# Conv stage: channel-block pairs stored with the low quarter first, only that quarter split in two parts, and the last three tap groups closed row by row

## The reference, cut to what matters

```python
def _L0_attn_a_ref(x, block_values, cols, rows):      # x: (2, 512, 256); 128 blocks of 64 x 64 x 16 taps
    xb = x.reshape(batch, n_block_row, bs, t)          # 8 blocks of 64 channels
    x_unfold = xb[:, cols].reshape(batch, n_blocks * bs, t)
    o = conv_general_dilated(x_unfold, W, padding=[(ks - 1, 0)], feature_group_count=n_blocks)
    y = zeros(...).at[:, rows].add(o)
...
x = x + _L0_attn_a_ref(_layernorm(x), block_values, cols, rows)
x = x + _L0_ffn_ref(_layernorm(x), ...)
x = x + _L0_attn_b_ref(_layernorm(x), ...)
x = x + _L0_ffn_ref(_layernorm(x), ...)
```

## Time and profile before

| what | value |
|---|---|
| median of 3 runs | 882.07 us (882.04 to 882.12) |
| profiled execution | 882.04 us, its span 880.2 us |
| PE, DVE, ACT, POOL busy | 99%, 60%, 48%, 36% of the span |
| granted TensorE clock | 1.000 over the span |
| the convolution ends (barrier L143) | 129.5 us from the start |
| f1 ends (barrier L598) | 345.5 us from the start |

### The profile page before, as it was taken

How to read it: one execution, slowest core, us unless ns; L and a number is a source line. 1 busy time by engine, 2 the same in 40 slices (tenths; PEclk the granted TensorE clock), 3 DMA queues, 4 the chain that set the end, 5 groups by cost and what they waited for, 6 DMA issues and landing times. The chain is left out here.

```text
span 880.2 us, 16767 instructions
## 1 busy us (share of the span) xinstructions
PE 870.3 (99%) x5626; PEld 774.1 (88%) x5626; DVE 531.5 (60%) x1361; ACT 426.4 (48%) x947; POOL 317.9 (36%) x290
## 2 busy tenths in 40 slices
PE   9999999999999999999999999999999999999998
PEld 7999778888888888889989998998997888888887
DVE  5999997333333337887588768858877433333334
ACT  3522256443343334777477557747746434334332
POOL 5211013555655654231122213111112556555562
PEclk9999999999999999999999999999999999999999
DMA  8999402111111112000100000000001111111111
GB/s 337 338 372 385 164 18 92 55 36 54 45 44 54 37 36 69 7 25 2 37 0 24 36 0 24 0 0 1 1 1 63 46 54 36 54 54 36 54 36 48
DMA packets 25553, 61.00 MB, mean 69 GB/s; under 512 B 3298, under 2 KB 10916, under 8 KB 25508
## 3 DMA queue, kind: packets, MB, share of 16 engines
q1 hardware_dynamic: 23204, 47.82, 15.8%
q0 software_dynamic: 2304, 12.58, 3.8%
HBM read 59.35 MB, written 1.05 MB: 69 GB/s over the span
## 5 line engine op out<-in xcount | busy, mean ns | idle before, releaser
L956 DVE TENSOR_TENSOR f_h<-f_scaled,bank 128x512 f32<-128x512 f32 (+1 forms) x90 | 60.8, 676 | 179.4 <-POOL f_scaled L822 166.9
L737 ACT ACTIVATE f_h_hi<-f_h 128x512 fp32r<-128x512 f32 (+2 forms) x102 | 63.7, 624 | 187.3 <-DVE f_h L956 187.3
L822 POOL TENSOR_TENSOR f_scaled<-f_act,f_gate_rows 128x512 f32<-128x512 f32 x80 | 102.9, 1286 | 116.3 <-ACT f_act L730 115.9
L1056 PE MATMUL bank<-f_xt_hi,f_w_hi 128*128 128x512 f32 (+2 forms) x360 | 141.1, 392 | 0.5 <-ACT f_xt_hi L134 0.3
L1056 PE MATMUL bank<-f_xt_hi,f_w_lo 128*128 128x512 f32 (+2 forms) x360 | 141.3, 393 | 0.0
L963 DVE TENSOR_TENSOR f_h_lo<-f_h,f_h_hi 128x512 fp32r<-128x512 f32 (+2 forms) x102 | 71.8, 704 | 70.7 <-ACT f_h_hi L737 70.2
L1274 ACT ACTIVATE at_prob<-bank,at_sbias,at_qrs 128x512 f32<-128x512 f32 (+3 forms) x128 | 77.6, 617 | 72.6 <-DVE at_sbias L1467 72.6
L1056 PE MATMUL bank<-f_xt_lo,f_w_hi 128*128 128x512 f32 (+2 forms) x360 | 110.9, 390 | 0.0
L1069 PE MATMUL bank<-f_w_lo,f_h_hi 128*128 128x256 f32 (+1 forms) x352 | 99.6, 283 | 0.0
L1069 PE MATMUL bank<-f_w_hi,f_h_lo 128*128 128x256 f32 (+1 forms) x352 | 99.6, 283 | 0.0
L1069 PE MATMUL bank<-f_w_hi,f_h_hi 128*128 128x256 f32 (+1 forms) x352 | 99.3, 282 | 0.0
(11 more groups left out here) (219 smaller groups left out, 2094.1 us busy)
## 6 DMA issues: line engine op xcount, KB each, us to landing
cv_raw<-in_wconv SPq DMA_DIRECT2D x26, 512.0 KB, 6.5
cv_shared<-in_wtaps POOLq DMA_DIRECT2D x16, 768.0 KB, 7.4
f_wraw<-in_w SPq DMA_DIRECT2D x42, 256.0 KB, 2.6
xn<-in_wconv SPq DMA_DIRECT2D x14, 512.0 KB, 6.6
f_wraw<-in_w SPq DMA_DIRECT2D x42, 128.0 KB, 2.5
at_wraw<-in_wqkv SPq DMA_DIRECT2D x3, 768.0 KB, 4.5
at_oraw<-in_wo SPq DMA_DIRECT2D x4, 512.0 KB, 3.5
X<-in_x_tiles SPq DMA_DIRECT2D x2, 512.0 KB, 8.0
```

The lines of the kernel that those rows point to most:

```text
L737: a.activation(h_hi[slot][0:rows, cols], h_f[half][0:rows, cols], ACT.Copy).then_inc(s["h_hi_done"], 1)
L822: g.tensor_tensor(scaled[half][:], act[half][:], gate_rows[:, half * HALF:(half + 1) * HALF], ALU.mult).then_inc(s["scaled_done"], 1)
L956: v.tensor_tensor(h_f[half][0:rows, cols], src[half][0:rows, cols], pu[half][0:rows, cols], ALU.mult)\
L1056: mm = t.matmul((pg, pu)[gu][half][0:out_rows, :], w, x, start=q == 0, stop=q == 3 * KH - 1)
```

## The change

Pairs get a new order, `pair_index`: low quarter (column < 4 and row < 4) first, as pairs 0 to 15. The one-hot matrix and the addresses of the adds follow it (for the addresses DVE computes four small operations over 128 numbers more, in group 0). For groups 0 to 4, ACT now copies a bank in two operations: 384 elements of the upper pairs into `full`, unsplit, then 128 elements into `ws_hi`; DVE subtracts 128 elements. For groups 5 to 7, `acc` is laid out by group first, an add covers 3 x 32 elements instead of 96, and only the low pairs are split, in two pieces per group (rows 0 and 1 of the accumulators), all three groups' first pieces ahead of all second ones. Each group from 5 on has a slot of its own. The unused path would do unsplit matmuls.

TensorE's tail is written anew: after group 4 accumulators 2 and 3 are closed; then for accumulator 0 the products of groups 5, 6, 7, close; then the same for accumulator 1, close. `following["normalize"]` stands ahead of `add_rows(2)`. `keep_busy` issues 1 matmul instead of 6 at the end of the convolution, and 1 instead of 4 at the end of f1.

```diff
-        BANK_BLOCKS = ((2, 4, 4, 4, 4, 4, 8, 4), (4, 4, 4, 4, 4, 4, 8, 8), (4, 4, 4, 4, 4, 4, 2, 14))
+        BANK_BLOCKS = ((4, 4, 4, 4, 4, 4, 6, 6), (5,) * 8, (6, 6, 6, 6, 6, 6, 2, 0))
...
+        def pair_index(c, row):
+            return c * (NCB // 2) + row + (c >= NCB // 2) * (NW // 4) + (row >= NCB // 2) * (NLOW - NCB // 2)
...
                 for q in banks:
                     a.wait_ge(s["summed"], st * SB + q + 1)
-                    a.activation(ws_hi[slot][:, :, q * OB:(q + 1) * OB],
-                                 ps[q % BANKS][:].rearrange("p (w o) -> p w o", o=OB), ACT.Copy)\
-                     .then_inc(s["ws_hi_done"], 1)
+                    sums, cols = ps[q % BANKS][:].rearrange("p (w o) -> p w o", o=OB), slice(q * OB, (q + 1) * OB)
+                    a.activation(full[slot][:, :, cols], sums[:, NLOW:NW, :], ACT.Copy)
+                    a.activation(ws_hi[slot][:, :, cols], sums[:, 0:NLOW, :], ACT.Copy).then_inc(s["ws_hi_done"], 1)
...
-                    part = slice(k * DROW // 2, (k + 1) * DROW // 2)
-                    dst = acc[:, bass.ds(pairs[n], 1), part].rearrange("p a f -> p (a f)")
-                    v.tensor_tensor(dst, dst, raw_d[d % 3][:, n, part], ALU.add).then_inc(s["added"], 1)
+                    part = slice(k * BS // 2, (k + 1) * BS // 2)
+                    dst = acc[:, :, bass.ds(pairs[n], 1), part].rearrange("p e a f -> p e (a f)")
+                    src = raw_d[d % 3][:, n, :].rearrange("p (e f) -> p e f", e=ND)[:, :, part]
+                    v.tensor_tensor(dst, dst, src, ALU.add).then_inc(s["added"], 1)
...
             for n in range(2):
                 add_rows(v, n)
             following["variances"](v, 0)
+            following["normalize"](v, 0)
             add_rows(v, 2)
-            following["normalize"](v, 0)
...
+            def convolve_added():
+                with t.If(flag != 0):
+                    ...
+                for r in (2, 3):
+                    close(r)
+                for r in range(GC // 2):
+                    for st in range(NPE, NST):
+                        t.wait_ge(s["ws_lo_done"], piece_of(st, r) + 1)
+                        for c in range(NCB // 2):
+                            products(st, c, r)
+                    close(r)
...
-            for st in range(NPE - 1, NST - 1):
-                convolve(st)
-            convolve_last(NST - 1)
-            keep_busy(t, pm, ps[1], 6)
+            convolve_last_banks()
+            convolve_added()
+            keep_busy(t, pm, ps[1], 1)
...
-                keep_busy(t, pm, ps[1], 4)
+                keep_busy(t, pm, ps[1], 1)
```

More of the change, by code:

```diff
@@ L155, in conv_phase @@
         raw += [sb(f"raw{i}", [P, CHUNK], F32)[:] for i in range(2, RING)]
[L156 to L158 removed]
+        NLOW = NW // 4
+        ws_hi, ws_lo = ([pm["held"][:, (2 * i + part) * NLOW * BS:(2 * i + part + 1) * NLOW * BS]
+                         .rearrange("p (w o) -> p w o", w=NLOW) for i in range(2)] for part in range(2))
+        ws_hi += [sb(f"ws_hi{i}", [P, NLOW, BS], F32R)[:] for i in range(2, ND + 1)]
+        ws_lo += [sb(f"ws_lo{i}", [P, NLOW, BS], F32R)[:] for i in range(2, ND + 1)]
+        full = [sb(f"full{i}", [P, NW - NLOW, BS], F32) for i in range(2)]
+        acc = sb("acc", [P, ND, NW, BS], F32)
         colrow = sb("colrow", [P, 2], I32)
@@ L444, in _ @@
                     done, pairs = end, more
-            for st in range(NPE, NST):
-                low_sums(st)
+            for r in range(GC // 2):
+                for st in range(NPE, NST):
+                    low_sums(st, r)
             for n in range(2):
@@ L491, in high_products @@
             def high_products(st):
-                with t.If(flag != 0):
-                    t.wait_ge(s["ws_lo_done"], splits_before(st + 1))
-                    for c in range(NCB):
-                        for r in range(GC):
-                            if c >= NCB // 2 or r >= GC // 2:
-                                products(st % 2, c, r, st * 2)
-            def finish_products(st):
-                t.wait_ge(s["ws_lo_done"], splits_before(st + 1))
-                high_products(st)
+                for c in range(NCB):
+                    for r in range(GC):
+                        if c >= NCB // 2 or r >= GC // 2:
+                            w, e = pair_index(c, 2 * r), st - NPE
+                            if st < NPE:
+                                sums = full[st % 2][:, w - NLOW:w - NLOW + 2, :]
+                            else:
+                                sums = acc[:, e, w:w + 2, :]
+                            for x in (xc_hi, xc_lo):
+                                t.matmul(ps[4 + r][:], sums.rearrange("p c o -> p (c o)"), x[:, c, :, bass.ds(st * 2, D)].bitcast(F32),
+                                         start=False, stop=False)
@@ L502, in finish_products, with close @@
+            def finish_products(st):
+                t.wait_ge(s["ws_lo_done"], (st + 1) * SB)
+                with t.If(flag != 0):
+                    t.wait_ge(s["ws_lo_done"], (st + 1) * SB)
+                    high_products(st)
                 t.matmul(ps[4][:, 0:1], zeros[:, 0:P], zeros[:, 0:1], start=False, stop=False)\
                  .then_inc(s["ws_free"], 1)
-            def convolve(st):
-                for n, (c, r) in enumerate(LOW_PAIRS):
-                    if st >= NPE and r == 0 and c in (0, NCB // 4):
-                        t.wait_ge(s["ws_lo_done"], splits_before(st) + (1 if c == 0 else LOW_PIECES))
-                    elif n == 0:
-                        t.wait_ge(s["ws_lo_done"], splits_before(st + 1))
-                    products(st % 2, c, r, st * 2)
-                finish_products(st)
+            def close(r):
+                t.matmul(ps[4 + r][:], zeros[:, 0:P], zeros[:], start=False, stop=True).then_inc(s["conv_done"], 1)
```

95 lines of the change are left out of this document (50 added, 45 removed).

## The result

| | before | changed |
|---|---|---|
| median of 14 runs each | 882.02 us (881.08 to 882.20) | 884.36 us (882.89 to 885.11) |
| profiled execution, its span | 882.04, 880.2 | 885.11, 883.3 |
| granted TensorE clock | 1.000 | 0.998 |

The ratio is 1.0029, with a 95% interval of 1.0020 to 1.0037: slower by 0.29%, where 878.9 (877.7 to 880.7) was forecast.

The account below looks back on a forecast made before the run. TensorE, busy in 99% of the span at full clock, was taken as the bound; 882.04 less 2.56 (tail and first barrier) and 0.63 (second barrier) gave 878.85, stated as 878.9 us, range 877.7 to 880.7.

Parts of the forecast that it names:

- so a subtraction costs DVE some 0.4 less: Groups up to 4: DVE's subtraction falls from 512 elements, 0.68 long, to 128 elements, 0.29 long.
- plus about 0.1 for loading addresses, fits 2.50: Group 3: subtraction and ten adds take 2.14 a bank, plus this load term, within TensorE's 2.50 per bank.
- 0.21 + 12 x 0.193 + 0.08 = 2.6, just over 2.50: Group 4: DVE's time per bank for subtraction, twelve adds and address loading, against TensorE's 2.50.
- The ladder with 8.0 to landing: Raw chunks 5 to 15 followed at 8.0 us landing: adds end 102.5, last subtraction 102.8, group 4's products start 102.85.
- Rival 2: Ahead of group 4's products: later chunks put DVE further behind, S near 105.5, time 881.5; chance 0.13.
- S: Start of group 4's products on TensorE; forecast 102.85, 0.57 later than before.
- Rival 5: Clock falls at a barrier with fewer fillers; 7 us at half clock would cost 3.5; chance 0.02.
- 24 products 5.72, one-column matmul 0.04, two closings 0.24: Convolution's tail from S: first terms of the sum that puts the last closing at S + 23.24, 126.1.
- PE's wait for the split of `acc` (1.56): Behind group 4's products: this wait for DVE's first split would go, as the adds end earlier.
- rival 4: Adds of 3 x 32 cost more, group 4 has no slack; 0.2% slower needs S near 108; chance 0.04.
- The gain is eaten at S = 106: Within rival 4: an extra 0.034 per add delays group 4's products until no gain is left.
- rival 1: Raw chunks arrive in time, group 4's products start at 101.93, 0.9 less: 877.9 to 878.0; chance 0.28.

Follow-up runs that it names:

- run 2: Changed kernel with the adds' addresses loaded 16 at a time instead of 8, so 8 loads instead of 16: 884.60 us, ratio 1.0030.
- run 12: Changed kernel with each address load of groups 2 to 4 moved ahead of the subtraction it stood behind: 884.18 us, ratio 1.0029.
- run 5: Changed kernel with four buffers instead of three for the raw chunks of groups 5 to 7: 881.77 us, ratio 0.9997.
- run 6: Changed kernel with the first 8 blocks' addresses loaded once and used for all 16 chunks (wrong pairs for chunks 1 to 15): 879.39 us, ratio 0.9971.
- run 7: Changed kernel with addresses loaded only once (wrong pairs for chunks 1 to 15) and four chunk buffers: 879.47 us, ratio 0.9972.
- Run 3: Changed kernel with 18 matmuls on zeros ahead of TensorE's wait for group 4's last subtraction: 883.06 us, ratio 1.0016.
- run 1: Changed kernel with group 4 taking 4 blocks of adds per bank, 2 at the seventh, and 12 behind the last bank's subtraction: 878.66 us, ratio 0.9965.
- run 10: run 1 with one branch over 192 matmuls for groups 4 to 7 and group 4's one-column matmul left out: 877.86 us, ratio 0.9954.
- run 4: Changed kernel with the branch over 144 unused matmuls of groups 5 to 7 split into three over 48 each: 887.52 us, ratio 1.0058.
- run 9: run 1 with the long branch and closings of accumulators 2 and 3 moved behind group 5's first 12 products: 879.30 us, ratio 0.9972.
- run 8: Kernel before the change with one filler matmul instead of four at the end of f1: 881.20 us, ratio 0.9993.

## Why the prediction was wrong

**The step that failed** is the one that dates the end of the adds: "so a subtraction costs DVE some 0.4 less", taken together with "plus about 0.1 for loading addresses, fits 2.50" in group 3 and "0.21 + 12 x 0.193 + 0.08 = 2.6, just over 2.50" in group 4. The 0.1 was what a load shows beyond a subtraction of 0.68, and the change shortens that very cover. A bank with a load takes 0.70 + 12 x 0.193, about 3.0, and 3.05 in the trace, where the prediction had 2.6 and TensorE 2.50. The rows show this price load by load (sixteen waits for issue, 7.4 in all, where it was 0.3), run 2 that it goes by the addresses loaded, and run 12 that ahead of the subtraction it is the same. In run 5, where no chunk is waited for, it is by its rows about the 2.10 that are left. No run takes away the loads and nothing else: run 6, in which the wait is gone, has quicker adds as well.

**The chunks.** The ladder with 8.0 to landing was near (8.0 at the median). It gave a start of 102.85, the row is 106.70. Of the 3.85 between, 0.27 are start-up. Of the 4.38 of wait, run 5 wins 2.3 by taking the chunk waits (2.5 in total) away; run 7 takes them away where loads and address settings are gone, and wins nothing. So the late chunks cost something here because DVE had no time left for them. Rival 2's S near 105.5 was closer than the forecast's, by another mechanism.

**Two costs behind the wait that no term had.** With S near 105.5 rival 2 still said 881.5. What it lacks is, first, the clock: it fell behind the idle time, and 24 products took 7.01 instead of the 5.72 of the sum. Run 3, which keeps TensorE busy through the same wait, shows that it is this. Rival 5 had a falling clock, but at a barrier; and the rule cited there (*TensorE: Matmul & The Clock Gate* of the Trainium skill, "Why this matters for your kernels", no long idle gaps between bursts) should have been laid beside each wait that the rivals made. Second, the long branch, which holds two transfers of instructions: "24 products 5.72, one-column matmul 0.04, two closings 0.24" has no term for it, since eight such branches had cost 0.2 to 0.4 before. It held the closings up by 0.99 here, by 1.32 in run 1, and run 10 takes it off the path.

**Against the sum.** (The 0.27 of start-up is not the change's; see the last section.) The transposes were forecast at 127.05 and came at 133.27, 6.22 later: start-up 0.27, the wait 3.58, the clock 1.29, the branch 0.99, and 0.09 for the rest.

**What was right.** From the closings to the last closing it is 17.51; the prediction's 0.24 + 8.6 + 0.04 + 8.6 is 17.48. PE's wait for the split of `acc` (1.56) is gone. The last closing to the transposes is 1.02, forecast 0.95, and PE drains last. The second barrier gives back 0.65, forecast 0.63, and there the drains of both engines end together, at 348.3:

```profile
L624 DVEq DRAIN  x1: 1677/1677/1677, 346.6 to 346.6; - x1
L624 PEldq DRAIN  x1: 1352/1352/1352, 347.0 to 347.0; - x1
```

An add of 3 x 32 costs what one of 96 did, so rival 4, the only one headed slower, had the right place and the wrong mechanism. Its "The gain is eaten at S = 106" was well placed: the wait by itself, 3.58 on 878.85, makes 882.4, no change; the 2.28 of clock and branch made it slower. Run 1 is the change with slack ahead of the last subtraction: 878.66, where 878.9 stood. That the two are so close is luck, since the run has no wait at all (0.9 better, as in rival 1), and 1.3 of bare branch, which no term had, against it.

## What to carry over

- Before an instruction is made shorter, list what it covers on its own queue: a cost read from the trace as the difference between two gaps (0.69 and 0.60) is only what stands out from under the cover. Take the record of the hidden instruction (0.6) less the new cover (0.28): the trace then shows 0.35 to 0.42.
- A term for a wait on TensorE needs two more: what the clock does during it, and what of the queued work behind it had been covering (a branch, a drain).
- When a run leaves an instruction out to price it, count by line what else has gone: run 6 lost 15 loads and, unasked, 240 address settings.
- When a producer is just too slow for its consumer, leave it slack ahead of the last hand-over: twelve blocks moved behind the last bank were worth 5.7 us (884.36 to 878.66).

## What the runs showed of the hardware that I had not expected

- A register load on DVE takes 0.60 us at the median for 8 values and 1.10 for 16, and one already running covers it only to its own length: 0.28 of subtraction leaves 0.35 to 0.42 of a load bare, and so does an addition of 0.25 (0.41).
- Setting an address ahead of each add (57 ns a record) slows DVE's adds of 96 elements from 2.01 to 2.34 for twelve, 0.03 each (run 6 against the changed kernel), though the length of one add, 254 and 255 ns, shows nothing of it.
- The granted clock. Idle for 2.10 before the products, in the profiled execution of run 5, it stayed at 1.00; by the mean clocks it fell in seven of that run's ten executions, of which no trace is kept. With waits of 3.70 to 4.38 it fell to 0.50 in the traces of all four kernels that had one (the changed one, runs 2, 4 and 12), and again behind 3.27 of idle time in run 4. The way back differed: it was at 0.50 in the slices from 107 to 109 in the changed kernel, and in those from 105 to 111 in run 12, with the same work. So a wait of 4.38 cost 1.3 (24 products in 7.01) and one of 4.02 cost 2.4 (8.13 from 105.80 to 113.93). But slower products also cover the branch behind them: in run 12 only 0.26 lies between the one-column matmul and the closings, where the changed kernel has 1.03. That is why clock and branch are one bill, 2.28 in the changed kernel's trace and 2.63 in run 12's.
- A branch that jumps takes PE's queue 0.2 to 0.4 us where it jumps 48 or 72 matmuls by itself, 3.4 to 5.1 where it jumps 144 or 192, and 3.4 to 3.5 for the first and second of three short ones (run 4). The jump over most matmuls, 192, takes least of the long ones, 3.36. Where the end is bare, the next matmul comes up to 0.3 behind it, in run 4 0.4. The branch starts 1.9 behind the first of 24 products at full clock (105.36 and 107.3 in run 3), and 1.9 + 4.6 to 5.1 is 6.5 to 7.0, an estimate, against 5.7 of products: 0.8 to 1.3 bare, and it is 0.94 to 1.43 in the brackets of the runs at full clock. In run 2 the products take 8.39 at half clock; the branch ends at 108.9 + 4.6 = 113.5, ahead of them, and nothing is bare. What fills the long ones: inside every branch of 4.6 to 5.1 two transfers of instructions of 16 KB start, inside every one of 3.4 to 3.9 (both in run 4, those in runs 9 and 10) one, and inside the short branches over the unused pairs none, but for one of 0.37 in run 8. So the length goes with the blocks brought in, and not with the matmuls jumped. The record doesn't say which engine a block is for, and it is no proof: no run changes the blocks and nothing else. The Trainium skill, *Advanced Engine Details and Errata*, gives a compare-and-branch at about 108 ns ("Control Flow Timing"); no branch over the unused pairs is that short here, 205 ns being the least. Its section "ISA Cache" says that instructions are cached in lines of 256. The trace has as many weight loads as matmuls (5616 of each), so 144 matmuls are 288 instructions, more than a line, and 48 are 96. That agrees with the transfers inside the long jumps, and with two of three short ones in a row leaving a line; why 192 matmuls needed one block and 144 mostly two, it doesn't tell.
- Start-up. The first 11 matmuls on zeros take 4.88 in the profiled executions of the kernel before and of the changed one, 3.88 in run 1, and values between in other runs, in code that is the same there, and move all that follows by up to 1 us. The 0.27 between the two kernels arises just behind them, in five more matmuls on zeros that start at 6.13 in both: they take 1.77 in the changed kernel and 1.25 before, in the same code, and the first sum starts at 7.74 and 7.39. That is why places in different traces are compared here from the one-column matmul on. What sets this pace was not looked into; the windows give a clock of 1.00 there.
